# Attention and LPBQ feed-forward on one core: the last output projection begun by heads, the up stage on another bank pair, the sums of the down weights taken in the gate stage, two VectorE forms rewritten

## The reference, cut to what matters

```python
# attention: 16 heads of 32; rotary embedding on q and k; causal softmax
q = rope(heads(layernorm(x) @ Wq.T + bq)); k = rope(heads(ctx @ Wk.T + bk)); v = heads(ctx @ Wv.T + bv)
x = x + merge(softmax(causal(q @ k.T / sqrt(32))) @ v) @ Wo.T + bo
# feed-forward: weights in 4-bit blocks of 32, activations in 16 bits with one scale per tensor
y = act_qdq(layernorm(x))
up = act_qdq(y @ lpbq(w_up).T); gate = act_qdq(y @ lpbq(w_gate).T)      # 1536 inner features
gate = act_qdq(gate * fixed_u16(sigmoid(gate)))
x = x + act_qdq(gate * up) @ lpbq(w_down).T
```

## Time and profile before

| | |
|---|---|
| median of three runs | 1534.3 us |
| profiled execution | 1533.25 us |
| its span | 1531.4 us |
| PE busy | 1378.5 us (90%) |
| DVE busy | 1185.7 us (77%) |
| ACT busy | 966.0 us (63%) |
| POOL busy | 340.1 us (22%) |
| mean granted PE clock | 0.958 of full |
| HBM traffic | 144.51 MB read, 82.84 MB written |

### The profile page before, as it was taken

The page is one execution under the profiler, slowest core; times in us unless marked ns, Lnnn a source line. Parts: engine busy times, 40 slices in busy tenths (PEclk is TensorE's granted clock), DMA queues, the critical chain, the costliest instruction groups (busy, mean ns, idle before and its releaser), DMA issues.

```text
span 1531.4 us, 24407 instructions
## 1 busy us (share of the span) xinstructions
PE 1378.5 (90%) x9198; PEld 775.2 (51%) x9198; DVE 1185.7 (77%) x1794; ACT 966.0 (63%) x2030; POOL 340.1 (22%) x325
## 2 busy tenths in 40 slices
PE   4899999999999999969999998999999106999998
PEld 3566676666666666634444443444444002444443
DVE  6778888888888888748878885888899798566541
ACT  6788888888988888754422223999788784212210
POOL 1354455554545454420111110000000000000000
PEclk9899999999999999979999999999999657999999
DMA  6111111111121211132333333666689999666522
GB/s 245 39 56 56 63 70 61 62 67 70 70 84 70 70 56 56 35 106 109 129 108 128 117 117 117 233 243 247 236 308 329 414 411 367 217 212 223 197 96 83
DMA packets 93413, 228.94 MB, mean 149 GB/s; under 512 B 8560, under 2 KB 8688, under 8 KB 90352
## 3 DMA queue, kind: packets, MB, share of 16 engines
q1 hardware_dynamic: 92288, 220.04, 40.4%
q10 hardware_dynamic: 1008, 7.34, 1.2%
HBM read 144.51 MB, written 82.84 MB: 148 GB/s over the span
## 4 chain that ended last, share of the span: by engine, by line
PE 32%; DVE 8%; ACT 6%; DMA 5%; issue 3%; SPq 0%; POOL 0%; ACTq 0%; DVEq 0%
PE ffn_banks L1233 16%; PE ffn_banks L1218 16%; DVE qg L1518 3%; ACT qg L1329 2%; DMA ffn_ring<-gates_dram 2%; DVE ffn_peaks L1414 2%; DMA ffn_wide<-ups_dram 1%; DMA signs_dram<-qg 1%; ACT ffn_rest L1277 1%; ACT ffn_ring L1333 1%; DVE ffn_rest L1516 1%; DMA ffn_ring<-ups_dram 1%; DVE ffn_ring L1501 1%; ACT ffn_wide L1358 1%; DVE ffn_rest L1500 0%
## 5 line engine op out<-in xcount | busy, mean ns | idle before, releaser
L1218 PE MATMUL ffn_banks<-ffn_wide,ffn_rest 128*128 128x512 f16 x2304 | 502.3, 381 | 8.0 <-DVE ffn_rest L1452 4.3
L1218 PEld LDWEIGHTS ffn_banks<-ffn_wide,ffn_rest 128*128 128x128 f16 x2304 | 226.0, 98 | 284.1 <-issue 14.0
L1233 PE MATMUL ffn_banks<-ffn_rest,ffn_wide 128*128 128x512 f16 x1152 | 251.5, 382 | 83.0 <-DVE ffn_wide L1557 83.0
L1233 PEld LDWEIGHTS ffn_banks<-ffn_rest,ffn_wide 128*128 128x128 f16 x1152 | 113.2, 98 | 221.2 <-issue 87.0
L658 ACT ACTIVATE qg<-score_banks,neg_max 128x128 f32<-128x128 f32 (+1 forms) x512 | 208.0, 452 | 18.3 <-DVE neg_max L530 18.3
L1368 ACT ACTIVATE ffn_u_steps<-ffn_ring,ffn_scales 128x1024 int16<-128x1024 f32 x48 | 55.1, 1148 | 158.8 <-DMA ffn_ring<-ups_dram 146.5
L1277 ACT ACTIVATE ffn_rest<-ffn_banks,ffn_row_back 128x1024 f32<-128x1024 f32 x72 | 79.5, 1105 | 108.8 <-PE ffn_banks L1218 97.1
L432 POOL TENSOR_TENSOR qg<-qg,per_sum 128x512 f32<-128x512 f32 x64 | 82.5, 1290 | 270.2 <-DVE per_sum L534 270.2
L434 POOL TENSOR_TENSOR qg<-qg,per_sum 128x1024 f32<-128x1024 f32 x64 | 134.0, 2094 | 0.0
L658 ACT ACTIVATION_READ_ACCUMULATOR qg<-score_banks,neg_max 128x1 f32 x512 | 122.5, 240 | 0.0
L665 ACT ACTIVATE pt<-ring_banks 128x512 f32<-128x512 f32 x128 | 70.5, 614 | 48.2 <-PE ring_banks L792 47.2
(11 more groups left out here) (194 smaller groups left out, 2691.4 us busy)
## 6 DMA issues: line engine op xcount, KB each, us to landing
ups_dram<-ffn_rest SPq DMA_DIRECT2D x48, 512.0 KB, 3.8
ffn_ring<-ups_dram SPq DMA_DIRECT2D x48, 512.0 KB, 5.6
gates_dram<-ffn_rest SPq DMA_DIRECT2D x24, 512.0 KB, 2.8
ffn_ring<-gates_dram SPq DMA_DIRECT2D x24, 512.0 KB, 4.5
signs_dram<-qg SPq DMA_DIRECT2D x24, 512.0 KB, 4.1
ffn_wide<-ups_dram SPq DMA_DIRECT2D x12, 1024.0 KB, 17.5
qg<-signs_dram SPq DMA_DIRECT2D x24, 512.0 KB, 10.4
ffn_rest<-w_parts_dram SPq DMA_DIRECT2D x36, 256.0 KB, 4.1
```

Of the source, the lines that this page charges most:

```text
L1218: last = pe.matmul(banks[:, pair_of(s), half, :], w[:, m % 2, wp, c, :], xq[:, xp, n, c, :], start=(k == 0), stop=(k == 3 * DC - 1))
L1233: last = pe.matmul(down_banks[:, g % 2, t, :], oq[:, g % 2, op, m, t * P:(t + 1) * P], w_down[:, wp, wk, c], start=(start and k == 0), sto ...
```

## The change

**Last projection.** Oa is split. Ob does chunks 0 and 1 of a tile and waits only until head g of the last group has its exponentials, by a new semaphore `last_exped` that ACT raises after heads 0 and 1; it stands where Oa stood. Oc does chunk 2 of both tiles and stands behind the last PT.

**Up stage.** `pair_of` starts the up pieces at pair 0; the wait for the last weight unit moves from the first up piece to the fourth.

**Sums of the down weights.** sumd, its six loads, MX and scale of column 13 go from the attention. In the gate stage one buffer serves two sets: the 12 down units, summed by ACT behind pieces 3, 4 and 5, and the 12 up units, loaded after that and summed behind pieces 9, 10 and 11. POOL joins each set ahead of the first unit that needs it (units 0 and 12), DVE scales it at that unit. `unit_slot` becomes `PIECES + 2 + u * 5 // 3`: units start at piece 6 instead of 4, and the last stays at piece 44.

**VectorE forms.** The addition in rope and the scaling of the block maxima in wqa become `scalar_tensor_tensor`; the second takes its floor from a new small buffer.

```diff
-PE_AFTER[BATCH - 1, "PV", 2] = [("Oa", 0, BATCH - 1), ("Oa", 1, BATCH - 1)]
+PE_AFTER[BATCH - 1, "PV", 2] = [("Ob", 0, BATCH - 1), ("Ob", 1, BATCH - 1)]
+PE_AFTER[BATCH, "PT", 3] = [("Oc", 0, BATCH - 1), ("Oc", 1, BATCH - 1)]
...
-                    dve.tensor_tensor(qk[:, g], turns[:, 0], sin_turned[:, :, :], ALU.add).then_inc(rotated, 1)
+                    dve.scalar_tensor_tensor(out=qk[:, g], in0=turns[:, 0], scalar=1.0, in1=sin_turned[:, :, :], op0=ALU.mult,
+                                             op1=ALU.add).then_inc(rotated, 1)
...
-                    link(dve.tensor_scalar(step[:, :], block_max[:, :], 1.0 / WMAX, STEP_FLOOR, ALU.mult, ALU.max))
+                    link(dve.scalar_tensor_tensor(out=step[:, :], in0=block_max[:, :], scalar=1.0 / WMAX, in1=step_floor[:, :],
+                                                  op0=ALU.mult, op1=ALU.max))
...
+                        if s == BATCH * GROUPS - 1 and h < TT:
+                            last.then_inc(last_exped, 1)
...
-                if name == "Oa" or name == "O" and i == BATCH - 1:
-                    chunks = range(GROUPS - 1) if name == "Oa" else range(GROUPS - 1, GROUPS)
-                    if name == "Oa":
-                        pe.wait_ge(exped, BATCH * GROUPS)
+                if name in ("Ob", "Oc") or name == "O" and i == BATCH - 1:
+                    chunks = {"Ob": range(2), "Oc": range(2, 3), "O": range(3, 4)}[name]
+                    if name == "Ob":
+                        pe.wait_ge(last_exped, g + 1)
...
-    return PIECES + u * 7 // 4
+    return PIECES + 2 + u * 5 // 3
...
-UP_SUMS = 3
-UP_SUM_SLOT = 8
+SUMS = 3
+SUM_SLOTS = (PIECES - 1, PIECES + 5)
...
-            return s % 3 if s < NP else (s - NP + 3) % 4
+            return s % 3 if s < NP else (s - NP) % 4
...
+            def load_set(z):
+                if z > 0:
+                    sp.wait_ge(set_summed, SUMS * z)
+                at = IC + unit_of(z * IC)
+                sp.dma_start(set_raw.rearrange("p k (m o) -> p (k m) o", o=D),
+                             io["ffn_w"][at:at + IC].rearrange("m p o -> p m o")).then_inc(set_in, 16)
+
+            load_set(0)
             for s in range(NP):
+                if s == SUM_SLOTS[1] - 2:
+                    load_set(1)
...
-                elif s == NP:
+                elif s < NP + 3:
+                    pe.wait_ge(staged, s - 2)
+                elif s == NP + 3:
                     pe.wait_ge(w_split, 2 * IC)
-                elif s < NP + 4:
-                    pe.wait_ge(staged, s - 3)
...
             for u in range(2 * IC):
+                if u % IC == 0:
+                    z = u // IC
+                    pool.wait_ge(set_summed, SUMS * (z + 1))
+                    pool.partition_all_reduce(set_total[:, z, :], set_sums[:, z, :], P, REDUCE.add).then_inc(set_joined, 1)
                 pool.wait_ge(w_rounded, u + 1)
...
-                if unit_at[u] >= UP_SUM_SLOT + UP_SUMS and unit_at[u - 1] < UP_SUM_SLOT + UP_SUMS:
-                    pool.wait_ge(up_summed, UP_SUMS)
-                    pool.partition_all_reduce(up_total[:, :], up_sums[:, :], P, REDUCE.add).then_inc(up_joined, 1)
```

More of the change, by code:

```diff
@@ L41 @@
 GATE_LAG = 3
-DOWN_SCAN, DOWN_SCANS = 9, 6
-JOINS = ((0, 3), (3, 2)) + tuple((5 + n, 1) for n in range(9))
+JOINS = ((0, 3), (3, 2)) + tuple((5 + n, 1) for n in range(8))
 SUM_SCALE = 2.0 ** -17
@@ L142 @@
     ACT_AFTER[i, SUM_AT[1][0], SUM_AT[1][1]] = [("sumc", 0, 2 * k + 1)]
-for k in range(DOWN_SCANS):
-    ACT_AFTER[DOWN_SCAN + k, "pte", 1] = ACT_AFTER.get((DOWN_SCAN + k, "pte", 1), []) + [("sumd", k, 0)]
 DVE_AFTER = {(i, "max", 3): [("scale", 2 + k, 0)] for i, k in LATE_SETS}
-DVE_AFTER[DOWN_SCAN + DOWN_SCANS, "max", 2] = [("scale", 10, 0)]
-PE_AFTER[BATCH - 1, "PV", 2] = [("Oa", 0, BATCH - 1), ("Oa", 1, BATCH - 1)]
+PE_AFTER[BATCH - 1, "PV", 2] = [("Ob", 0, BATCH - 1), ("Ob", 1, BATCH - 1)]
+PE_AFTER[BATCH, "PT", 3] = [("Oc", 0, BATCH - 1), ("Oc", 1, BATCH - 1)]
 DVE_AFTER[BATCH - 1, "recip", 3] = [("dnorm", 3, BATCH - 1)]
@@ L158 @@
 for name, g, i in ACT_PLAN:
-    if name in ("sumw", "sumc", "sumd"):
-        for at in ((2 * g, 2 * g + 1) if name == "sumw" else (8 + i,) if name == "sumc" else (8 + BATCH + g,)):
+    if name in ("sumw", "sumc"):
+        for at in ((2 * g, 2 * g + 1) if name == "sumw" else (8 + i,)):
             if at != 2 * MK + 1:
@@ L252, in attend @@
         ident = keep["ident"]
[L254 removed]
+        Q_COL, K_COL, V_COL, O_COL = 0, 1, 3, 4
         def c_set(i):
@@ L262, in sums_of_column @@
         def sums_of_column(col):
-            if col == D_COL:
-                return [8 + BATCH + k for k in range(DOWN_SCANS)]
             if col in (Q_COL, K_COL, V_COL, O_COL):
```

92 lines of the change are left out of this document (38 added, 54 removed).

## The result

The changed kernel takes 1518.6 us, the median of four runs (1518.15 to 1519.55), against 1535.0 (1533.8 to 1536.0) for the kernel before, now with a fourth run beside the three: a ratio of 0.990, 95% interval 0.9888 to 0.9912. On a second chip five more runs gave 0.9902 (0.9886 to 0.9918). So the gain is 15 to 16 us; 13.7 was forecast (1520.6 us, range 1514.5 to 1528.0). The profiled execution took 1518.15 us, with a span of 1516.3: 15.1 us less than the one before.

The account below looks back on a forecast made before the run. PE was taken to bound the gate stage and most of attention, DVE the late up stage, then full DMA engines. Gains 6.2 + 2.0 + 4.3 + 1.5 - 0.3 = 13.7 us gave 1520.6 us, range 1514.5 to 1528.0.

Parts of the forecast that it names:

- Part 1: Seam of gate and up stage: with the first up piece on pair 0, PE runs on without idling; gain 6.2 us.
- Part 2: Last attention turn: column 13's product MX gone, saving PE's time on it and slow matmuls behind it; gain 2.0 us.
- The second half of the step: Last turn's projection: dropping MX also avoids the lower clock in the 12 matmuls behind it; 1.55 us.
- Part 3: End of attention: last projection split by heads, so the last transposes start 6.14 us earlier; gain 4.3 us, between 1.3 and 5.3.
- the low-clock case: Last transposes to last PV: at 1.2 GHz this stretch takes up to 6.4 us, gain only 2.1 or 1.3.
- 2.2 us is half of that, so full speed: PE's idle ahead of the last transposes: half the 4.27 and 4.47 us that lowered the clock, so leaning to full speed.
- Part 4: Attention turns: six sumd activations gone from ACT, 0.29 us each on the path; gain 1.5 us, bounds 0 and 6.7.
- Part 5: Gate stage: two sets of weight sums and POOL joins delay DVE about 3 us but never stop PE; cost 0.
- rival C: Gate stage: POOL's joins stop PE, at worst 14.3 us each, making the kernel 14.9 us slower, 1549.2 us; chance 4%.
- Part 6: Rope's addition and block maxima scaling: the new DVE forms are held by POOL like the old; cost 0.3 us.
- Rival B: Attention: the rewritten DVE forms escape POOL's holds, 8 us more gain, 1512.6 us; chance 7%.

Follow-up runs that it names:

- pair back: The changed kernel with only the up stage's bank change undone: the first up piece uses its former pair and waits for the last weight unit; 1524.8 us, ratio 0.9940.

## Why the prediction was right, point by point

- **Part 1 (forecast 6.2):** right. 6.12 at the seam, 5.8 with the part undone, and nothing of it lost on the way to the down stage, though DMA is as full behind the up stage (share 1.02) as in the earlier trace rows. The stretch gained 6.7 because the first two gate pieces took 12.72 us instead of 13.22, with a granted clock of 0.83 in them against 0.79.
- **Part 2 (2.0):** 1.5 in the pair of traces. The product's own 1.4 are sure. The second half of the step, that leaving it out avoids the lower clock behind it, failed in this trace: with the product gone, the clock had fallen already at the scores (0.81 us at 638.58 for what takes 0.50 at full clock). Over fourteen traces item 15 takes 38.6 us on average with the product and 35.1 without, a difference of 3.5; three traces are too few to say that this is the part's worth. Between 1.4 and 3.5 it stays open.
- **Part 3 (4.3, from 1.3 to 5.3):** right in mechanism. 3.55 in the pair, 3.2 with the part undone. The 6.0 us of earlier transposes came as forecast; the giving back was the low-clock case, 4.86 us to the last PV. The lean on "2.2 us is half of that, so full speed" had no ground: after the same 2.19 us both speeds are seen, the lower one in three of ten traces. Over all traces this stretch takes 31.6 us on average without the part (two) and 27.2 with it as it is (nine), a gain of 4.5; that the forecast's 4.3 lies so near is luck, as it rests on that lean.
- **Part 4 (1.5):** mis-sized; the six activations are worth 0.9. The forecast spread the 1.16 us between two stretches of four turns in one trace evenly over the turns and carried it to six. Two of the turns carry the whole cost, 0.45 us each, the last two none, and the other 0.26 us of the 1.16 is scatter: six turns without activations differ from trace to trace by up to 0.6.
- **Part 5 (0):** right in what it costs: PE did not wait from 700 us to the end of the gate stage, and rival C falls. The working had some 3 us of DVE's waiting at unit 12 and none at unit 0; measured are 2.0 and 1.6. It had priced the change back behind the first join like that of the earlier trace rows, 7.56 us, and POOL's multiply came 11.40 us after it.
- **Part 6 (-0.3):** the form makes no difference, so 0. Rival B was right about one thing: the holds do cost time. Removed altogether from rope's addition, they are worth some 2.6 us (2.8 in items 1 to 14), a third of the 8 that I gave that rival.
- **The rest:** the medians' gain (16.3) exceeds the sum (13.7) by 2.6 us, and no run gives that to a part. In the pair of traces 0.8 lie ahead of the first item and 1.8 behind the start of the down stage, where the code is the same; what the parts gained in that pair is less than forecast, 6.1 + 1.5 + 3.55 + 0.9 = 12.05. The second chip's ratio gives 15.0. So the closeness of the total to the measured time owes something to luck; the mechanisms of parts 1, 3 and 5 do not.

## What to carry to other kernels

A wait at a seam between stages pays in full when all that follows is released by work that moves with it; look at the start of the last stage to see whether it arrived. An off-path engine's long instruction can be cut into halves for the sake of a neighbour that is blocked until the instruction ends; this gave more than either rewritten form. And before a term below 2 us is read from one trace, take the same stretch from several: here single items differ by steps of 1.5 us from the clock alone, while a cost of 0.45 us in one item could be read clearly from fourteen traces, since that item is otherwise alike within 0.03 us.

## What the hardware showed that was not expected

The granted clock in the last item differs between executions of the same work. In the kernel with the pair back, the score products of group 3 come after the same idle time as in the changed kernel (638.58, above), 1.55 us against 1.56, and run at full clock (PE's timeline):

```profile
641.49 0.50 PE L760 MATMUL score_banks<-qg 32*128 32x128 f32 x8 [1.55 <-ACT qg L640]
```

Stretch 640 to 650 of that kernel, which holds these products, and of the changed one, where they begin 1.4 us ahead of it (length, PE busy and count, granted clock, DMA share, GB/s):

```profile
640.00:650.00 10.00, 8.51 (x64) 1.00 0.00 0
```

```profile
640.00:650.00 10.00, 10.00 (x80) 0.92 0.00 0
```

In the same way the stretch from item 0's marker to item 1's takes 41.4 us in six traces and 42.9 to 43.2 in eight; in seven of the eight the clock is below full between 90 and 110 us, in the eighth (pair back) it is full, and PE once waits 1.74 us for POOL where the changed kernel waits 0.22. What decides whether the clock falls was not settled.
